# Column sums of the attention weights: four products on quarters of TensorE's columns instead of two on halves

## The reference

```
x: 4 x 1024 x 256, 16 heads of 64
xn  = layernorm(x)
q, k, v = xn @ Wq, xn @ Wkv          # split into heads, rotary on the first 32 of 64 dims of q and k
sim  = q k^T * 64 ** -0.5             # per batch and head, 1024 x 1024
attn = softmax(sim)
out  = (attn @ v) @ Wout + bout
ffn  = fp4_linear(silu(fp4_linear(xn, w_gate)) * fp4_linear(xn, w_up), w_down)   # blockwise fp4 quantise/dequantise
return x + out + ffn
```

## Time and profile before

| | us |
|---|---|
| median of 3 runs | 1981.33 |
| lowest and highest of the 3 | 1979.59, 1981.44 |
| the profiled execution, its own time | 1980.87 |
| its span, first to last instruction | 1979.1 |
| busy PE / DVE / POOL / ACT in the span | 1879.4 / 1491.2 / 1392.3 / 823.2 |
| TensorE clock granted, mean | 0.977 |

### The profile page before, as it was taken

One profiled execution on the slowest core, in us unless ns is written; L12 is line 12 of the kernel. 1 busy time (PEld: TensorE's weight loads), 2 busy tenths in 40 slices (PEclk: granted clock), 3 DMA queues, 4 the chain that ended last, 5 costly groups with the idle time before them and its releaser, 6 DMA issues.

```text
span 1979.1 us, 28994 instructions
## 1 busy us (share of the span) xinstructions
PE 1879.4 (95%) x10916; PEld 1156.2 (58%) x10916; DVE 1491.2 (75%) x2032; ACT 823.2 (42%) x1078; POOL 1392.3 (70%) x640
## 2 busy tenths in 40 slices
PE   5979999949999999999999999999999999999879
PEld 4768899825555555555555555555555555555579
DVE  6969999777777777777777777777777777775444
ACT  4642333203444444444444444444444444444422
POOL 3754544406787878788787878788787878789933
PEclk9999999959999999999999999999999999999989
DMA  7640301110121131111122111112211111112565
GB/s 257 250 187 27 136 33 51 44 32 22 44 58 46 50 86 44 49 44 60 44 60 86 50 44 48 45 44 60 87 58 46 49 44 48 45 34 54 191 234 203
DMA packets 141563, 152.88 MB, mean 77 GB/s; under 512 B 41840, under 2 KB 97776, under 8 KB 141168
## 3 DMA queue, kind: packets, MB, share of 16 engines
q1 hardware_dynamic: 141424, 151.03, 24.2%
HBM read 95.95 MB, written 55.05 MB: 76 GB/s over the span
## 4 chain that ended last, share of the span: by engine, by line
PE 62%; DVE 20%; issue 6%; POOL 3%; DMA 1%; ACT 0%; SPq 0%; POOLq 0%; DVEq 0%
PE banks L994 17%; PE banks L1014 12%; PE banks L939 10%; PE banks L971 9%; PE banks L997 6%; DVE half_max L1067 3%; PE banks L1023 3%; PE banks L1486 3%; POOL acc L1189 3%; DVE q_lo L1112 2%; DVE k_lo L1112 2%; DVE h_scales L110 2%; DVE f_y L131 1%; DVE f_amax L109 1%; DVE f_y L134 1%
## 5 line engine op out<-in xcount | busy, mean ns | idle before, releaser
L1189 POOL TENSOR_TENSOR acc<-acc,prob 128x1024 f32<-128x1024 f32 x384 | 919.3, 2394 | 153.7 <-ACT prob L1215 125.2
L1067 DVE TENSOR_REDUCE half_max<-banks 128x2 f32<-128x1024 f32 x512 | 628.1, 1227 | 305.4 <-PE banks L971 305.4
L1215 ACT ACTIVATE prob<-banks 128x1024 f32<-128x1024 f32 x512 | 512.5, 1026 | 624.8 <-PE banks L997 624.8
L1014 PE MATMUL banks<-prob,v 128*64 128x512 f32 x2048 | 495.7, 605 | 0.0
L1189 POOL TENSOR_TENSOR acc<-prob,prob 128x1024 f32<-128x1024 f32 x64 | 152.7, 2386 | 180.8 <-ACT prob L1215 180.8
L1014 PEld LDWEIGHTS banks<-prob,v 128*64 128x64 f32 x2048 | 124.3, 136 | 240.4 <-issue 191.9
L971 PE MATMUL banks<-k_hi,q_hi 64*128 64x512 f32 x1024 | 235.8, 456 | 21.8 <-DVE half_max L1067 20.8
L939 PE MATMUL banks<-xT,wqk 128*128 128x512 f32 x768 | 218.3, 420 | 2.0 <-DVE k_lo L1112 2.0
L971 PEld LDWEIGHTS banks<-k_hi,q_hi 64*128 64x128 f32 x1024 | 98.3, 187 | 199.8 <-issue 150.7
L994 PE MATMUL banks<-q_hi,k_hi 64*128 64x512 f32 x1024 | 204.7, 395 | 1.3 <-ACT prob L1215 1.3
L994 PE MATMUL banks<-q_hi,k_lo 64*128 64x512 f32 x1024 | 203.5, 392 | 0.0
(11 more groups left out here) (121 smaller groups left out, 2204.2 us busy)
## 6 DMA issues: line engine op xcount, KB each, us to landing
v_scratch<-v_out SPq DMA_DIRECT2D x32, 512.0 KB, 2.6
wqk<-wp_scratch SPq DMA_DIRECT2D x32, 512.0 KB, 3.5
v<-v_scratch SPq DMA_DIRECT2D x32, 512.0 KB, 4.7
inv_rows<-inv_scratch SPq DMA_DIRECT2D x128, 128.0 KB, 3.3
o_scratch<-o_norm SPq DMA_DIRECT2D x64, 256.0 KB, 2.0
o_in<-o_scratch SPq DMA_DIRECT2D x8, 2048.0 KB, 12.1
xn_scratch<-p_xT SPq DMA_DIRECT2D x32, 256.0 KB, 2.9
xT<-xn_scratch SPq DMA_DIRECT2D x8, 1024.0 KB, 6.3
```

Source lines behind the costliest of these rows:

```text
L1014: ins = nc.tensor.matmul(o_ps[head * DH:(head + 1) * DH, :], v[s % 2][:, kt, at:at + DH], prob[n % SLOTS][:, head, :], start=kt == 0, stop ...
L1067: nc.vector.tensor_reduce(half_max[:, half % 2, :, t % GRP, part], m_ps[:, :, :], axis=AX.X, op=ALU.max, negate=True).then_inc(half_maxed, 1)
L1189: nc.gpsimd.tensor_tensor(acc[b][:, :, :], first, prob[n % SLOTS][:, :, :], ALU.add).then_inc(added, 1)
L1215: nc.scalar.activation(prob[n % SLOTS][:, :, :], s_ps[n % 2][:, :, :], ACT.Exp).then_inc(exp_done, 1)
```

## The change

`QUAD, QROWS, SUMS` are 4, 32 and 256. The weight tile `ones` becomes 128 x 32, and a column sum becomes four products of 256 moving columns, each on a quarter of TensorE's columns: product k takes head k // 2 and the queries' half k % 2, and its result stands on PSUM partitions 32k to 32k+31 in columns 0 to 255 of the bank. ACT copies 128 x 256, and SP stores the four rows of partitions 0, 32, 64 and 96, 256 numbers each, to the same place in DRAM in the same order. The semaphores, their waits and the order on every engine stay.

```diff
+QUAD, QROWS, SUMS = 4, P // 4, GCOL // 2
...
-    ones = small("ones", [P, DH], F32)
+    ones = small("ones", [P, QROWS], F32)
...
-    sum_rows = [late(f"sum_rows{i}", [P, GCOL], F32) for i in range(2)]
+    sum_rows = [late(f"sum_rows{i}", [P, SUMS], F32) for i in range(2)]
...
             pe.wait_ge(added, adds_before(2 * s + half + 1))
-            for head in range(2):
-                ins = nc.tensor.matmul(misc_ps[head * DH:(head + 1) * DH, :], ones[:, :], acc[half][:, head, :], start=True, stop=True)
+            for k in range(QUAD):
+                ins = nc.tensor.matmul(misc_ps[k * QROWS:(k + 1) * QROWS, 0:SUMS], ones[:, :],
+                                       acc[half][:, k // 2, k % 2 * SUMS:(k % 2 + 1) * SUMS], start=True, stop=True)
             ins.then_inc(misc_done, 1)
...
-            nc.scalar.activation(sum_rows[half % 2][:, :], misc_ps[:, :], ACT.Copy).then_inc(sums_copied, 1)
+            nc.scalar.activation(sum_rows[half % 2][:, :], misc_ps[:, 0:SUMS], ACT.Copy).then_inc(sums_copied, 1)
...
             sp.wait_ge(sums_copied, half + 1)
-            sp.dma_start(io["sum_scratch"][b], sum_rows[b][0:P:DH, :]).then_inc(sum_stored, 16)
+            sp.dma_start(io["sum_scratch"][b].rearrange("h (k c) -> (h k) c", k=2), sum_rows[b][0:P:QROWS, :]).then_inc(sum_stored, 16)
```

## The result

| | before | after |
|---|---|---|
| median, us | 1980.46 (4 runs, 1979.15 to 1981.44) | 1952.2 (4 runs, 1950.38 to 1952.73) |
| ratio | | 0.9856, 95% interval 0.9839 to 0.9873 |
| profiled execution: own time, span | 1980.87, 1979.1 | 1950.38, 1948.6 |

Faster by 1.4%, 28.3 us. The forecast was 24.5 us less and 1956.8 us, the range 1952.5 to 1969.5. The direction and the mechanism held; the time lies 0.3 us under the low end.

What follows compares the result with a forecast made beforehand. PE's sequence was taken to bound the kernel, with the column sum wholly on it: 59 x 0.41 = 24.2 us, plus 0.25 for the 60th, made 24.5 us less, 1956.8 us; range 1952.5 to 1969.5.

Steps and rivals of the forecast that it cites:

- The copy, the store and the inverse: Behind the column sum on ACT, SP and DVE: hidden, the store by 6 us of slack; only the last store on the chain.
- The wait for the low part: PE waits for DVE's q_lo or k_lo before 59 column sums; 0.21 us, claimed to stay as it is.
- the change of shape: PE going from 128*64 to 128*32 before the sum: 0.10 us, covered by the wait 59 times, paid at the 60th.
- the prediction's own sign (more than 0.64): L1023 starting over 0.64 us behind the last pair of values would show the change of shape isn't covered.
- the extra behind the first pair: Within the column sum on PE: 0.05 us beyond streaming, 0.48 between pairs instead of 0.43, kept in the new sum.
- The bound "pairs at most": Column sum on PE: if a pair is the widest that works, the sum takes 1.01 us, no gain.
- the first three rivals: Column sum: half side by side, 1969.5 us (10%); no effect, 1981.3 (10%); serial, slower, 2033 (5%).
- Gain 0.41 us each: Column sum on PE: 0.60 us instead of 1.01, times 59 sums, 24.2 us.
- the 0.66 of the forecast: From the 59th sum on: 0.41 us for that sum, 0.25 for the 60th, nothing for the last four.
- 60 x 0.48 from streaming alone: Column sums without start extra and staggered starts: 0.53 us each, gain 0.48, 28.8 us in all, giving 1952.5.

Runs made afterwards that it cites:

- the long copy: Changed kernel, but ACT copies all 512 columns of the bank again as before; 1950.86 us, ratio 0.9859 to before.
- the second set of eight: Changed kernel with the four products issued twice into the same places, 16 records instead of 8; 1976.46 us, ratio 0.9986 to before.
- two-abreast kernel: Changed kernel, but two products of 512 columns, one per head, each on a quarter of the columns; 1975.17 us, ratio 0.9979 to before.
- halves kernel: Changed kernel's four 256-column products, but on halves of TensorE's columns, ones 128 x 64, copy and store as before; 1977.68 us, ratio 0.9999 to before.
- the same swap on DVE: Changed kernel, DVE's low part issued ahead of the second maximum: rounds 2 and 6, 1945.73 us; from step 0, 1944.11; all four rounds then, 1951.44.

## Why the prediction was right, and where it was wrong

**Right: what bounds, and what hides.** PE's own sequence set the pitch, the sum lay wholly on it, and a shorter sum shortened each half step. The copy, the store and the inverse are hidden: the long copy changed nothing. The wait for the low part stayed and covered the change of shape: the sum starts 0.65 us behind the values against 0.64. By the prediction's own sign (more than 0.64) this is 0.01 too late. The means over the first 59 sums are 0.645 and 0.648 us in the two traces of before and 0.652 in both of the changed kernel, so under 0.01 of the 0.10 shows. Where no wait covers it, at the 60th sum, it costs the forecast 0.10. The timeline of the changed kernel there:

```profile
1765.94 0.60 PE L1015 MATMUL banks<-prob,v 128*64 128x512 f32 x2
1766.47 0.64 PE L1024 MATMUL banks<-acc,ones 128*32 128x256 f32 x8
1767.04 0.50 PE L972 MATMUL banks<-k_hi,q_hi 64*128 64x512 f32 x2
```

0.53 from the values to the sum, where a pair of values follows another after 0.43. In the kernel before, this sum took 0.95 and not 1.01: without a wait and a change of shape ahead of it, the extra behind the first pair isn't there.

**Right: side by side.** All four stream together, which no row of before could show. The bound "pairs at most" and the first three rivals fell with the two rounds of four 0.24 us apart, and the second set of eight at 0.43 settles it. The loss that the Trainium skill's TensorE: Matmul & The Clock Gate (Part 3) has for three column tiles, 2.38 times instead of 3, doesn't appear here with four: eight more records cost 0.43 us, what two rounds of 0.215 take. The 0.10 us agrees with the drain at a change of mode that the Trainium skill's TensorEngine Tiling (Key Properties) has, and the two versions with the low part first in rounds 2 and 6 show it too: 0.53 us from the values to the sum, 0.10 more than the 0.43 between pairs.

**Wrong: the size of the term, 0.41 us a half step.** The step that failed is the sum "Gain 0.41 us each" in the part on PE. It measured 0.47, and two things were mis-sized in it.

- *The sum itself*, put at 0.60 and measured at 0.57. The step at fault is the 0.05 us "extra behind the first pair", carried over unchanged. With a weight tile of 32 columns it is 0.03: 0.24 between the rounds less 0.215 of streaming. The two-abreast kernel shows it alone, 0.98 us against 1.01 with the same streaming. The sum itself so gained 0.44.
- *Outside the sum*, 0.03 us a half step that no term had. It comes with the kernels on quarters, not with the shorter copy or the number of records: the pitch falls by 0.03 to 0.04 more than the sum in the two-abreast and long-copy kernels, and not at all with halves. It lies in one place, the gap from a guess to the values in even rounds, first in the halves kernel, then in the changed one (timelines of PE):

```profile
1014.39 0.40 PE L972 MATMUL banks<-k_hi,q_hi 64*128 64x512 f32 x2
1014.72 0.65 PE L1015 MATMUL banks<-prob,v 128*64 128x512 f32 x2
```

```profile
1002.88 0.39 PE L972 MATMUL banks<-k_hi,q_hi 64*128 64x512 f32 x2
1003.19 0.65 PE L1015 MATMUL banks<-prob,v 128*64 128x512 f32 x2
```

0.33 and 0.31, and that twice a half step. The mean over all of these gaps between the first and the 59th sum, by the starts in the traces, is 0.332, 0.332 and 0.330 us in the three traces without quarters, and 0.317 in each of the eight with them. Twice 0.015 is the whole 0.03. Why a guess and values that have nothing to do with the sum come closer together is open. One rival was not tested: the eight kernels also share an `ones` of half the width, and every tile allocated behind it lies 128 bytes further down in each partition. No run keeps the quarters and the old places, so the cause can be either.

So 58 intervals give 58 x 0.47 = 27.3 us, not 23.8. The other 1 us of the 28.3 is within the spread of the runs and isn't put down to a place. From the 59th sum on, the traces of before and after taken later differ by 1.1 us up to the 64th sum (92.16 against 91.04), then by 1.2 the other way to the end, about what the 0.66 of the forecast and the spread there allow.

**Wrong: the low end of the range, 1952.5.** It was 60 x 0.48 from streaming alone, counted from 1981.33. The gain measured, 28.3 to 28.5 us on both occasions, is inside the 28.8 of that bound. The start was not: 1981.33 was a median of three, and later sets of 9 to 19 runs have 1979.1 to 1979.6. A bound counted from the median of three needed another 2 us below it. The bound was also one of the sum alone, and the 0.03 us outside it was in no bound. Either alone would have left the time inside the range: without the 0.03 the time would be about 1953.9 us, and from a start of 1979.3 the low end would be 1950.5 (estimates from the figures above).

## What to carry to other kernels

A product whose result is one row repeated (sums over partitions by ones) needs no more than 32 columns of TensorE, and splitting its moving columns over four quarters halved the streaming against two halves here (0.86 to 0.43 us; the whole sum went from 1.01 to 0.57). It pays if PE sets the pace and the result's new places can be read as cheaply. Price such an edit from the starts of instructions, with what is paid once (weight load, change of array shape) apart from streaming, and look whether a wait already covers the change of shape. Set a range from more than three runs of the kernel that it starts from. Before changing the order on a second engine, compare what PE does behind the wait: the same swap on DVE gained 0.13 to 0.14 us a half step ahead of a 0.57 us sum and lost it ahead of a 0.26 us transpose.

## What the runs showed of the hardware that was not expected

Four fp32 products on quarters of the columns start within 0.02 us of each other and stream 256 columns each, two records a product, in two rounds 0.24 us apart. There is no loss against two abreast: a second set of eight records takes 0.43 us, where the same columns two abreast take 0.86. Records of 256 columns on the full width take 0.216 us each, as each round of that second set does. The extra at the start is smaller with the smaller weight tile, 0.05 us with 64 columns and 0.03 with 32, and it is absent where a sum on halves follows values without a wait (the 60th of before). And the guess-to-values gap elsewhere in the round fell from a mean of 0.33 us to 0.317 in every kernel that used quarters and the smaller `ones`; which of the two does it, and how, these runs don't show.
